# Ninety-six unused bytes at the end of SBUF, under a causal attention kernel in fp32 pairs

## The chip, the cores and the metric

The kernel runs on one core of one Trainium2 chip. The metric is the device time of one launch in microseconds (us), as the median of several runs. The engines are PE (matmuls, with PEld for its weight loads), DVE (VectorE), ACT (ScalarE), POOL (GpSimd) and SP (SyncE, which here only issues DMAs).

## The reference

The input is one sequence of 2048 tokens of 512 values. After a layer norm, a multi-head latent attention with 16 heads is computed, and a gated linear layer with eight low-rank experts; the two results are multiplied and added to the input:

```python
xn = _layernorm(x, axis=-1)
s = _L0_attn_ref(xn, W_DQ, W_UQ, W_QR, W_DKV, W_UK, W_UV, W_KR, W_O)   # 16 heads, 128 + 64 rotary, causal, scores clipped to +-80
g = _silu(_L0_ffn_ref(xn, weight, lora_A, lora_B, router_w))          # base layer + top 2 of 8 experts of rank 16
x = x + s * g
```

Inside the attention, per head: scores = q k^T with q and k of 128 + 64 values, softmax over the keys up to the token's own, times v (the latent of 128 values stands for both k and v), then the output projection W_O.

## The kernel before, in words

Every fp32 operand of a matmul is split into a high and a low part (names ending in `_h` and `_l`), and each product is three matmuls: high by high, high by low, low by high.

Three phases follow each other.

1. `prepare` (the first 150 us or so) normalizes x, makes latents, keys, values and the linear layer. Its buffers lie on the left side of SBUF and are given back at its end.
2. The sweep, in `attend_and_combine`. The sixteen tiles of 128 query tokens are taken in eight couples of 256 tokens, and each couple in two units of eight heads: unit n = 2m + par is couple m, heads 0 to 7 (par 0) or 8 to 15 (par 1). A unit holds its queries as `q_h`, `q_l`, `rot_hh`, `rot_l0`, each 128 x 2048, and walks over its key tiles: first the diagonal tile (CORNER), then the second diagonal tile (LATE), then 2m full tiles (FULL). Each key tile is one pair of halves (four heads each). In a half PE writes the scores, ACT takes the exponential (line 1415), DVE clips it (1540), ACT casts the high part (1421), DVE subtracts for the low part (1558) and adds to the row sums (1553), and PE multiplies with the values. PE works one pair ahead with the scores.
3. The projection (`project`, lines 1361 to 1363): 16 tiles of tokens, each 16 heads x 3 matmuls of 128 x 512, from about 1232 us to the end.

In FULL pairs the matmuls run as two at once, on the upper and the lower 64 rows of the array. One half is 15 such slots: nine for scores (line 1242, moving operands `q_h`, `q_l`, `q_h`, `rot_hh`, `rot_l` and then `q_h`, `q_l`, `q_h`, `rot_hh`) and six for the values (line 1264, moving operands `prob_h`, `prob_l`, `prob_h`, twice). CORNER and LATE use whole-array matmuls (lines 1212 to 1224 for scores, 1283 to 1287 for values). All of these stream 512 fp32 columns, 2048 bytes of each partition, except in LATE, where some stream 256.

```python
for n, (upper, lower, moving) in enumerate(blocks):
    for r, keys_of in enumerate((upper, lower)):
        c = 1 - r if crossed else r
        mm = pe.matmul(score_ps[:, half, c * 512:(c + 1) * 512], keys_of[ROWS[r], :],
                       moving[par][ROWS[r], half * HW + c * 512:half * HW + (c + 1) * 512],
                       start=n == 0 and not crossed, stop=n == len(blocks) - 1 and crossed)
```

The buffers of the two parities lie on different sides of SBUF. Those of par 0 (`q_h0`, `q_l0`, `rot_hh0`, `rot_l00`, `total0`) are in the class `Top`, on the right side; those of par 1 (`q_h1` and so on) are on the left. `merged_l`, one of the two moving operands of the projection, takes the place of the four query buffers of par 0 when the sweep ends; `merged_h` is on the left.

```python
q_h, q_l, rot_hh, rot_l0 = [top.q_h, q_h1], [top.q_l, q_l1], [top.rot_hh, rot_hh1], [top.rot_l0, rot_l01]
merged_h, merged_l = by_heads(keep.merged_h[:, :], DIM), by_heads(top.merged_l[:, :], DIM)
```

The right side is filled downwards from byte 229344 of each partition, which is 96 past a multiple of 128.

Of the kernel before, what the change touches and what calls it, by code (L numbers as in the profile page):

```python
# [18 lines left out]
F32 = mybir.dt.float32  # L19
F32R = mybir.dt.float32r  # L20

P = 128
# [51 lines left out]


WO_FIRST = 13


def homes(nc, ctx, side, words, sets):


    made = []
    for tensors in sets:
        with ExitStack() as lent:
            made.append([lent.enter_context(nc.sbuf_tensor(name, [P, width], dt, side=side)) for name, width, dt in tensors])
    ctx.enter_context(nc.sbuf_tensor("home_of_" + sets[0][0][0], [P, words], F32, side=side))
    return made


class Persistent:  # L90


    def __init__(self, nc, ctx):
        def sb(name, shape, dt):
            return ctx.enter_context(nc.sbuf_tensor(name, shape, dt))

        ((self.cos, self.sin, self.qr_h, self.qr_l), (self.wo_first,),
         (self.rows_h, self.rows_l, self.scale, self.x_in)) = homes(nc, ctx, "left", 2 * (SEQ + CT) + 4 * GT, (
            (("cos", SEQ + CT, F32), ("sin", SEQ + CT, F32), ("qr_h", 2 * GT, F32R), ("qr_l", 2 * GT, F32R)),
            (("wo_first", WO_FIRST * DIM, F32),),  # L100
            (("rows_h0", HQ, F32R), ("rows_l0", HQ, F32R), ("scale0", HQ, F32), ("x_in0", DIM, F32))))
        ((self.absorb_h, self.absorb_l, self.cq_h, self.cq_l),
         (self.merged_h, self.x_in1)) = homes(nc, ctx, "left", 2 * HQ + 2 * (SEQ + CT), (
            (("absorb_h", HQ, F32R), ("absorb_l", HQ, F32R), ("cq_h", SEQ + CT, F32R), ("cq_l", SEQ + CT, F32R)),
            (("merged_h", HEADS * DIM, F32R), ("x_in1", DIM, F32))))
        self.causal = sb("causal", [P, CT], F32)
        self.ones = sb("ones", [P, 32], F32)


class Top:  # L110
# [2 lines left out]

    def __init__(self, nc, ctx):

        self.head_rows = ctx.enter_context(nc.sbuf_tensor("head_rows", [P, HQ], F32, side="right"))
        self.sums = ctx.enter_context(nc.sbuf_tensor("sums", [P, 512], F32, side="right"))
        (self.q_h, self.q_l, self.rot_hh, self.rot_l0), (self.merged_l,) = homes(nc, ctx, "right", 4 * HQ, (
            (("q_h0", HQ, F32R), ("q_l0", HQ, F32R), ("rot_hh0", HQ, F32R), ("rot_l00", HQ, F32R)),
            (("merged_l", HEADS * DIM, F32R),)))  # L120
        (self.total,), (self.rows,) = homes(nc, ctx, "right", HQ, ((("total0", HQ, F32),), (("rows0", HQ, F32),)))
# [701 lines left out]
def attend_and_combine(nc, keep, top, keys, values, turned, w_uv, w_o, heads_out, sums_out, inverses, x, linear, out):  # L823

    ctx = ExitStack()
    with ctx:
# [3 lines left out]
        def sem(name):  # L830
# [18 lines left out]
            (*((f"prod{n}", 512, F32) for n in range(4)), ("rot_f", 2 * 512, F32), ("rot_hl", 4 * 512, F32R)),  # L849
            (("wo_rest", (HEADS - WO_FIRST) * DIM, F32), ("uv", HEADS * LAT, F32)),  # L850
            (("rows1", HQ, F32), ("scale1", HQ, F32), ("lin_in0", DIM, F32), ("gate0", DIM, F32))))
# [8 lines left out]
        def by_heads(ap, width):  # L860

            return ap.rearrange("p (h n) -> p h n", n=width)

        wo_parts = [by_heads(keep.wo_first[:, :], DIM), by_heads(wo_rest[:, :], DIM)]
        wo = [wo_parts[h // WO_FIRST][:, h % WO_FIRST, :] for h in range(HEADS)]
        uv = by_heads(uv_flat[:, :], LAT)
# [859 lines left out]
```

## Time and profile before

| | |
|---|---|
| Median of 3 runs | 1421.35 us (1419.82 to 1422.22) |
| The profiled execution's own time | 1420.26 us |
| Its span, first to last instruction | 1418.7 us |
| Granted TensorE clock over the span | 0.994 |
| Busy: PE, PEld | 1381.4 us (97%), 1147.4 us (81%) |
| Busy: DVE, ACT, POOL | 1146.3 us (81%), 782.1 us (55%), 125.1 us (9%) |
| HBM read, written | 125.83 MB, 48.50 MB, 123 GB/s over the span |

Busy time is the union of an engine's instructions. Matmuls are pipelined, so that the one that follows starts while the one before is still in its recorded 0.39 us; the step from start to start says how fast PE goes, and the busy share doesn't.

### The profile page before, as it was taken

What the parts mean: (1) busy time and instruction counts of PE and PEld (TensorE: products, weight loads), DVE (VectorE), ACT (ScalarE), POOL (GpSimd) and SP (SyncE); (2) the same over time, 40 slices, a digit from 0 to 9 for tenths busy, and PEclk for the clock granted to TensorE, in tenths of its full rate; (3) what the DMA queues carried; (4) which work ended last, traced back from release to release, by engine and by line L of the source; (5) the groups of instructions that cost most, each with busy time, mean ns of one, the idle gap of its engine ahead of it and who ended that gap; (6) DMA issues with size and microseconds to landing.
All of it is one profiled execution on the core that took longest, in us unless ns stands there. A gap on an engine that the chain in (4) does not pass through costs nothing.

```text
span 1418.7 us, 27675 instructions
## 1 busy us (share of the span) xinstructions
PE 1381.4 (97%) x9810; PEld 1147.4 (81%) x9810; DVE 1146.3 (81%) x1339; ACT 782.1 (55%) x861; POOL 125.1 (9%) x175
## 2 busy tenths in 40 slices
PE   7999689999999999999999999999999999999998
PEld 6888568778888888888888889888899688878887
DVE  7666378898898898988889898898788888967664
ACT  4232367666666666666566665666665656533221
POOL 0000111101101101010010100111100011022121
PEclk9999899999999999999999999999999999999999
DMA  8322665645435423333242422444412233166552
GB/s 304 121 88 101 176 190 152 177 131 160 119 94 141 120 95 91 123 84 120 66 119 85 116 99 63 122 151 140 131 56 63 67 109 118 52 199 172 169 158 89
DMA packets 110769, 174.91 MB, mean 123 GB/s; under 512 B 9608, under 2 KB 65160, under 8 KB 108168
## 3 DMA queue, kind: packets, MB, share of 16 engines
q1 hardware_dynamic: 93880, 108.99, 25.1%
q0 software_dynamic: 16016, 63.80, 15.7%
q10 hardware_dynamic: 832, 1.57, 0.5%
q8 instruction: 26, 0.43, 0.1%
q14 instruction: 15, 0.12, 0.0%
HBM read 125.83 MB, written 48.50 MB: 123 GB/s over the span
## 4 chain that ended last, share of the span: by engine, by line
PE 74%; DVE 8%; ACT 3%; DMA 3%; issue 1%; POOL 0%; ACTq 0%; SPq 0%; DVEq 0%; POOLq 0%
PE score_ps L1242 29%; PE out_ps L1264 19%; PE score_ps L1361 3%; PE score_ps L1362 3%; PE score_ps L1363 3%; DVE prob_l L1558 2%; PE out_ps L1283 1%; ACT prob_h L1421 1%; PE out_ps L1284 1%; PE out_ps L1287 1%; PE score_ps L1212 1%; DMA rot_l<-turned 1%; DVE prob L1545 1%; DVE prod L1517 1%; PE score_ps L1213 1%
## 5 line engine op out<-in xcount | busy, mean ns | idle before, releaser
L1421 ACT CAST prob_h<-prob 128x1024 fp32r<-128x1024 f32 (+1 forms) x288 | 289.8, 1006 | 236.1 <-DVE prob L1540 188.7
L1558 DVE TENSOR_TENSOR prob_l<-prob,prob_h 128x1024 fp32r<-128x1024 f32 (+1 forms) x288 | 335.9, 1166 | 39.6 <-ACT prob_h L1421 38.2
L1415 ACT ACTIVATE prob<-score_ps 128x1024 f32<-128x1024 f32 (+1 forms) x288 | 281.8, 979 | 148.8 <-PE score_ps L1242 99.3
L1242 PE MATMUL score_ps<-q_h,key_slot 64*128 64x512 f32 x1792 | 363.7, 391 | 0.0
L1264 PE MATMUL out_ps<-prob_h,value_slot 64*128 64x512 f32 (+1 forms) x1792 | 348.7, 377 | 1.8 <-DMA value_slot<-values 1.0
L1553 DVE TENSOR_TENSOR total<-total,prob 128x1024 f32<-128x1024 f32 (+1 forms) x256 | 294.7, 1151 | 0.0
L1540 DVE TENSOR_SCALAR prob<-prob 128x1024 f32<-128x1024 f32 x224 | 155.1, 692 | 72.0 <-ACT prob L1415 71.7
L1264 PEld LDWEIGHTS out_ps<-prob_h,value_slot 64*128 64x128 f32 x1792 | 178.3, 184 | 38.2 <-DVE prob_l L1558 6.6
L1242 PEld LDWEIGHTS score_ps<-q_h,key_slot 64*128 64x128 f32 x1792 | 178.2, 184 | 30.6 <-issue 5.0
L1242 PE MATMUL score_ps<-q_l,key_slot 64*128 64x512 f32 x896 | 181.1, 390 | 0.0
L1242 PE MATMUL score_ps<-rot_hh,key_slot 64*128 64x512 f32 x896 | 180.9, 389 | 0.0
L1264 PE MATMUL out_ps<-prob_l,value_slot 64*128 64x512 f32 (+1 forms) x896 | 174.7, 375 | 0.0
L1361 PE MATMUL score_ps<-merged_h,rows_h 128*128 128x512 f32 x256 | 101.1, 395 | 0.4 <-DVE rows_l L1568 0.4
L1362 PE MATMUL score_ps<-merged_l,rows_h 128*128 128x512 f32 x256 | 101.0, 395 | 0.0
L1242 PEld LDWEIGHTS score_ps<-rot_hh,key_slot 64*128 64x128 f32 x896 | 88.9, 184 | 14.3
L1363 PE MATMUL score_ps<-merged_h,rows_l 128*128 128x512 f32 x256 | 100.3, 392 | 0.0
L1264 PEld LDWEIGHTS out_ps<-prob_l,value_slot 64*128 64x128 f32 x896 | 89.3, 185 | 12.6
L1242 PEld LDWEIGHTS score_ps<-q_l,key_slot 64*128 64x128 f32 x896 | 89.0, 184 | 10.3
L1469 ACT CAST rows_h<-rows 128x1024 fp32r<-128x1024 f32 x32 | 33.7, 1052 | 109.9 <-DVE rows L1562 108.7
L1242 PE MATMUL score_ps<-rot_l,key_slot 64*128 64x512 f32 x448 | 90.3, 389 | 0.0
L1545 DVE SCALAR_TENSOR_TENSOR prob<-prob,causal 128x1024 f32<-128x1024 f32 (+1 forms) x64 | 61.0, 953 | 16.5 <-ACT prob L1415 16.2
L1507 DVE TENSOR_TENSOR q_l<-score_ps,q_h 128x1024 fp32r<-128x1024 f32 x32 | 37.8, 1219 | 27.8 <-ACT q_h L1386 27.8
(210 smaller groups left out, 2000.5 us busy)
## 6 DMA issues: line engine op xcount, KB each, us to landing
key_slot<-keys SPq DMA_DIRECT2D x144, 256.0 KB, 2.7
value_slot<-values SPq DMA_DIRECT2D x144, 128.0 KB, 2.3
rot_hh<-turned POOLq DMA_DIRECT2D x30, 512.0 KB, 6.2
heads_rows<-head_rows POOLq DMA_DIRECT2D x15, 1024.0 KB, 9.7
turned<-rot_hl POOLq DMA_DIRECT2D x14, 1024.0 KB, 5.2
rows<-heads_rows SPq DMA_DIRECT2D x28, 512.0 KB, 5.8
rot_l<-turned POOLq DMA_DIRECT2D x30, 256.0 KB, 7.7
x_in<-in_x SPq DMA_DIRECT2D x16, 256.0 KB, 2.7
```

The lines of the kernel that those rows point to most:

```text
L1242: mm = pe.matmul(score_ps[:, half, c * 512:(c + 1) * 512], keys_of[ROWS[r], :], moving[par][ROWS[r], half * HW + c * 512:half * HW + (c + ...
L1264: mm = pe.matmul(out, values_of[ROWS[r], :], moving, start=False, stop=False)
L1361: pe.matmul(sum_ps[par], rows_h[par][:, h, :], merged_h[:, h, :], start=(h == 0), stop=False)
L1362: pe.matmul(sum_ps[par], rows_h[par][:, h, :], merged_l[:, h, :], start=False, stop=False)
L1363: mm = pe.matmul(sum_ps[par], rows_l[par][:, h, :], merged_h[:, h, :], start=False, stop=(h == HEADS - 1))
L1415: nc.scalar.activation(prob[half][:, 0:width], score_ps[:, half, 0:width], ACT.Exp, scale=QK_SCALE).then_inc(exp_done, 1)
L1421: nc.scalar.copy(prob_h[half][:, 0:width], prob[half][:, 0:width]).then_inc(high_done, 1)
L1507: nc.vector.tensor_tensor(q_l[par][:, cols], score_ps[:, half, :], q_h[par][:, cols], ALU.subtract).then_inc(q_split, 1)
L1540: nc.vector.tensor_scalar(p, p, P_MIN, P_MAX, ALU.max, ALU.min).then_inc(clipped, 1)
L1545: nc.vector.scalar_tensor_tensor(out=heads, in0=heads, scalar=P_MIN, in1=limit, op0=ALU.max, op1=ALU.min).then_inc(clipped, 1)
L1553: nc.vector.tensor_tensor(sums, sums, by_head(half, kind), ALU.add).then_inc(summed, 1)
L1558: nc.vector.tensor_tensor(p_l, p, p_h, ALU.subtract).then_inc(split, 1)
```

## The change

The class `Top` reserves 24 fp32 words (96 bytes) per partition at the very end of the right side, before its other buffers. Nothing reads or writes them.

```diff
 WO_FIRST = 13
+EDGE = 24
...
     def __init__(self, nc, ctx):
 
+        ctx.enter_context(nc.sbuf_tensor("edge", [P, EDGE], F32, side="right"))
         self.head_rows = ctx.enter_context(nc.sbuf_tensor("head_rows", [P, HQ], F32, side="right"))
```

Every buffer on the right side then begins 96 bytes lower. The instruction lists of the two built programs are the same on every engine and in the same order, with the same waits; only the addresses of these buffers differ. The addresses, as the two builds place them (bytes in a partition), beside those of the left side that work with them:

| buffer | before | modulo 128, 256 | after | modulo 128, 256 |
|---|---|---|---|---|
| `head_rows` | 221152 | 96, 224 | 221056 | 0, 128 |
| `q_h0` | 210912 | 96, 224 | 210816 | 0, 128 |
| `q_l0` | 202720 | 96, 224 | 202624 | 0, 128 |
| `rot_hh0` | 194528 | 96, 224 | 194432 | 0, 128 |
| `rot_l00`, `merged_l` | 186336 | 96, 224 | 186240 | 0, 128 |
| `total0`, `rows0` | 178144 | 96, 224 | 178048 | 0, 128 |
| `q_h1`, `q_l1`, `rot_hh1`, `rot_l01` (par 1) | 87296 + 8192 k | 0, 0 | same | 0, 0 |
| `prob_h`, `prob_l`, `key_slot`, `value_slot` | | 0, 0 | same | 0, 0 |
| `merged_h` | 43136 | 0, 128 | same | 0, 128 |
| `w_h`, `w_l` in `prepare`, columns of chunk c | | 32 c | same | 32 c |
| `b_h`, `b_l` in `prepare` | 183936, 185984 | 0, 128 | same | 0, 128 |

## Rows read from the trace of the kernel before

**Rows 1.** The page, parts 1 and 2: busy us per engine, and granted clock by slices.

```profile
PE 1381.4 (97%) x9810; PEld 1147.4 (81%) x9810; DVE 1146.3 (81%) x1339; ACT 782.1 (55%) x861; POOL 125.1 (9%) x175
...
PEclk9999899999999999999999999999999999999999
```

**Rows 2.** The page, part 4: share of the chain that ended last, by engine.

```profile
PE 74%; DVE 8%; ACT 3%; DMA 3%; issue 1%; POOL 0%; ACTq 0%; SPq 0%; DVEq 0%; POOLq 0%
```

**Rows 3.** Busy us by stretch: PE, PEld, DVE, ACT, POOL, granted clock, DMA share, GB/s.

```profile
816.00:894.00 78.00, 77.97 (x676) 69.76 (x674) 69.65 (x71) 47.55 (x47) 1.00 (x1) 1.00 0.24 78
913.00:990.00 77.00, 76.88 (x681) 62.77 (x681) 68.99 (x72) 47.70 (x48) 11.28 (x20) 1.00 0.49 155
1290.00:1400.00 110.00, 110.00 (x477) 89.38 (x477) 73.83 (x71) 26.97 (x30) 23.35 (x10) 1.00 0.57 166
```

**Rows 4.** Exponentials (L1415) of units 12, 13, 14, 15: ns min/median/max, first and last start.

```profile
L1415 ACT ACTIVATE prob<-score_ps x10: 593/1026/1030, 797.0 to 832.4; 128x1024 f32<-128x1024 f32 x8, 128x512 f32<-128x512 f32 x2
L1415 ACT ACTIVATE prob<-score_ps x18: 1025/1027/1028, 835.8 to 894.9; 128x1024 f32<-128x1024 f32 x18
L1415 ACT ACTIVATE prob<-score_ps x10: 592/1026/1029, 898.3 to 933.5; 128x1024 f32<-128x1024 f32 x8, 128x512 f32<-128x512 f32 x2
L1415 ACT ACTIVATE prob<-score_ps x18: 1023/1027/1029, 936.9 to 994.5; 128x1024 f32<-128x1024 f32 x18
L1415 ACT ACTIVATE prob<-score_ps x18: 1026/1027/1031, 1024.7 to 1084.0; 128x1024 f32<-128x1024 f32 x18
L1415 ACT ACTIVATE prob<-score_ps x18: 1026/1029/1031, 1149.9 to 1207.7; 128x1024 f32<-128x1024 f32 x18
```

**Rows 5.** Timeline of PE in unit 12 (par 0), one half: start, duration us.

```profile
849.99 0.42 PE L1242 MATMUL score_ps<-q_h,key_slot 64*128 64x512 f32 x2
...
853.48 0.42 PE L1242 MATMUL score_ps<-q_h,key_slot 64*128 64x512 f32 x2
```

**Rows 6.** Timeline of PE in unit 13 (par 1), one half.

```profile
950.74 0.39 PE L1242 MATMUL score_ps<-q_h,key_slot 64*128 64x512 f32 x2
...
954.14 0.39 PE L1242 MATMUL score_ps<-q_h,key_slot 64*128 64x512 f32 x2
```

**Rows 7.** Timeline of PE where the last values follow on a projection tile.

```profile
1243.12 0.40 PE L1362 MATMUL score_ps<-merged_l,rows_h 128*128 128x512 f32 x1
...
1243.58 0.39 PE L1283 MATMUL out_ps<-prob_h,value_slot 128*128 128x512 f32 x1
...
1244.28 0.39 PE L1283 MATMUL out_ps<-prob_h,value_slot 128*128 128x512 f32 x1
...
1246.09 0.39 PE L1287 MATMUL out_ps<-prob_h,value_slot 128*128 128x512 f32 x1
```

**Rows 8.** Matmuls of line 1362 from 1271 us on: ns min/median/max, first and last start.

```profile
L1362 PE MATMUL score_ps<-merged_l,rows_h x208: 392/393/398, 1270.6 to 1414.2; 128*128 128x512 f32 x104
```

**Rows 9.** Costliest DVE groups, 919 to 996 us: busy us, mean ns, idle us before.

```profile
L1558 DVE TENSOR_TENSOR prob_l<-prob,prob_h 128x1024 fp32r<-128x1024 f32 x23 | 28.2, 1225 | 0.5 <-ACT prob_h L1421 0.5
L1553 DVE TENSOR_TENSOR total<-total,prob 128x1024 f32<-128x1024 f32 x22 | 26.8, 1218 | 0.0
L1540 DVE TENSOR_SCALAR prob<-prob 128x1024 f32<-128x1024 f32 x23 | 15.9, 692 | 6.3 <-ACT prob L1415 6.3
```

**Rows 10.** Timeline of PE in `prepare`, the matmuls that stream `b_h` and `b_l`.

```profile
76.42 0.40 PE L415 MATMUL base_ps<-b_h,turn_h 128*128 128x512 f32 x1
76.66 0.40 PE L416 MATMUL base_ps<-b_h,turn_l 128*128 128x512 f32 x1
...
78.29 0.40 PE L417 MATMUL base_ps<-b_l,turn_h 128*128 128x512 f32 x1
```

**Rows 11.** Casts into `q_h` of all units: ns min/median/max, first and last start.

```profile
L1386 ACT CAST q_h<-score_ps x32: 1002/1028/1042, 151.9 to 1006.9; 128x1024 fp32r<-128x1024 f32 x32
```

**Rows 12.** Landing of the `rot_l` gather: into par 1 (issued 369 us), into par 0 (428 us).

```profile
DMA to landing us min/median/max: 7.6/7.8/7.9
...
DMA to landing us min/median/max: 7.8/8.0/8.2
```

## The prediction, made before the changed kernel was run

> **What bounds the kernel now.** I read the page first. PE is busy for 97% of the span, DVE for 81% and the others less, and the clock is granted in full but for the beginning [rows 1]. The chain that ended last is PE for 74% of the span; DVE is the next with 8% [rows 2]. So the time of most of the kernel is the number of matmuls times the step from one to the next, and I looked for a difference in that step that could go with an address.
>
> The kernel holds an experiment of its own. Units of par 0 and of par 1 do the same work on the same shapes; the queries of par 0 lie on the right side, at 96 past a multiple of 128, and those of par 1 on the left, at multiples of 256. The stretches of unit 12 (par 0) and unit 13 (par 1) both have the full clock of 1.00, the higher of the two levels, 2.4 GHz, and PE is busy in all of both [rows 3]. Yet a half of unit 12 takes 853.48 - 849.99 = 3.49 us [rows 5] and one of unit 13 954.14 - 950.74 = 3.40 us [rows 6]. A half is 15 slots, so the step is 0.2325 us against 0.2267 us. It isn't one lucky half: over 17 halves the exponentials follow each other every (894.9 - 835.8) / 17 = 3.476 us in unit 12 and (994.5 - 936.9) / 17 = 3.388 us in unit 13, and it comes again as (1084.0 - 1024.7) / 17 = 3.488 and (1207.7 - 1149.9) / 17 = 3.400 us in units 14 and 15 [rows 4]. The difference is 0.088 us per half in both pairs of units.
>
> What else could differ between the units? DVE and ACT have the same work in both (69.65 and 68.99 us of DVE in stretches of 78 and 77 us), and par 1 has the busier DMA and is the faster one [rows 3]. What is left is where the moving operands of nine of the 15 slots lie. The values' slots, whose operands are the same in both units, must be slower too in par 0: the 0.09 us over 15 slots is more than I would place on any single one. I read this as a pace. PE falls into an even step of 0.2267 us when every operand begins at a round address, and never does when some don't.
>
> The place where the last values follow on a projection tile shows the pace setting in. The projection alternates `merged_h` (at 0 modulo 128) and `merged_l` (at 96) and steps by 0.23 us; the values that come right behind it (all at round addresses) start with such a step and then take eight steps from 1244.28 to 1246.09, 0.226 us each [rows 7]. These are whole-array matmuls, so the pace isn't a matter of the two at once. The projection itself never reaches it: 208 matmuls of line 1362 from 1270.6 to 1414.2, three slots each, give 143.6 / 621 = 0.2312 us per slot [rows 8], with PE busy in 110.00 of 110.00 us [rows 3].
>
> **The change part by part.** No instruction, wait or transfer is added, removed or moved, and the unused buffer costs nothing, as nothing touches it. All that can change is how long accesses to the moved buffers take.
>
> *Scores in par 0.* After the change the queries of par 0 are at 0 modulo 128. If their units then go as those of par 1, each half that PE paces gains 0.088 us. The first ten halves of a unit (CORNER, LATE and the first six of FULL) are nearly the same in both: from the first exponential to the eleventh 835.8 - 797.0 = 38.8 us in unit 12 and 936.9 - 898.3 = 38.6 in unit 13 [rows 4]. They are paced by the handing over between engines, and give 0.2 us per unit. Unit 2m has 4m halves of FULL; the first six don't count, which leaves 2, 6, 10, 14 and 18 for m = 2 to 6, or 50. Unit 14 is at its steady rate earlier, from the third or fourth half of FULL: 28 less 3, or 25. So 75 halves x 0.088 = 6.6 us, and 0.2 us for each of m = 3 to 7, or 1.0, where I take unit 14 as the others. Sum 7.6 us; I round it to 7.5. Were all 112 halves of FULL in par 0 paced by PE, it would be 9.9 us; that is the upper bound.
>
> What would be late next if PE is faster here is DVE. It has 1225 + 1218 + 692 = 3135 ns per half [rows 9], under the 3.40 us of a half in par 1, where the same work already goes at that rate; in that stretch it idles 6.3 us for ACT. So the gain isn't given back.
>
> *The projection.* 16 tiles x 48 = 768 slots. With both `merged_h` and `merged_l` at 0 modulo 128, and all weights too, the step can go from 0.2312 to 0.2267 us: 0.0045 x 768 = 3.5 us. PE is the pace there, DVE has 73.83 of 110 us and ACT 26.97 [rows 3].
>
> *The other users.* ACT and DVE write and read `q_h`, `q_l`, `total` and `head_rows` too. The 32 casts into `q_h`, half of them to each side of SBUF, lie between 1002 and 1042 ns [rows 11], so the side and the remainder are worth 40 ns each at most; they are inside the first halves of a unit, 14 of them to par 0 after the first, or 0.6 us if all of it were on the path. I take zero, nearest to the median of 1028. The gathers: the transfer of `rot_l` into par 1 lands after 7.6 to 7.9 us and that into par 0 after 7.8 to 8.2 [rows 12]. 0.2 us on two gathers that are on the chain early on is 0.4 at most; I take zero.
>
> The sum: 7.5 + 3.5 = 11.0 us, from the profiled execution's 1420.26 to 1409.3 us. That execution is 1.1 us under the median of the runs, so against the median of 1421.35 it is 1410.4 us.
>
> **What speaks against it: the rivals.** A change of 0.2% (2.8 us) is about what a measurement of this kernel can tell from none.
>
> *Nothing changes.* The parities also differ in the side of SBUF and in being at 0 or not modulo 256: every matmul of the trace that I saw in the even pace has all its operands at multiples of 256, and the right side is at 128 modulo 256 afterwards. The matmuls of `prepare` that stream `b_h` and `b_l`, both at 128 modulo 256, never settle in their groups of twelve: from 76.42 to 78.29 us eight steps of 0.234 us [rows 10], while the values in [rows 7] settled after three. This speaks for the rival; for my forecast speaks that their groups are short and come behind other shapes. The time would be 1421 us. The extra of the even step also hints at a granule: at 2.4 GHz 0.2267 us are 544 cycles for 512 columns, one more for each 16 columns or 64 bytes, an estimate worked out from [rows 6], and a multiple of 128 is a whole number of these.
>
> The Trainium skill (SBUF — State Buffer, Specifications) gives SBUF lines of 16 bytes, with a penalty for each crossing to a new line. 96 bytes are six whole lines, so by that rule no access crosses more lines before than after, and the time would stay. By that rule [rows 5] and [rows 6] would be alike too; the trace disagrees, with 3.49 against 3.40 us, as long as it is the address that sets them apart.
>
> *The sweep alone gains.* The projection has other weights for every matmul and another partner (`merged_h` at 128 modulo 256); if it doesn't settle, 1421.35 - 7.5 = 1413.9 us.
>
> *The projection alone gains.* If what counts is that all operands have the same remainder modulo 256, then `merged_h` and `merged_l` agree (128) and the queries of par 0 (128) and `prob` (0) don't: 1421.35 - 3.5 = 1417.9 us.
>
> *Slower.* A start at 128 modulo 256 could be the worse place. The longest steps that I found are in just such matmuls: 76.66 - 76.42 = 0.24 us [rows 10], against a mean of 0.2325. If the nine score slots of the 75 halves each took 0.24 in place of some 0.2335, it would be 9 x 75 x 0.0065 = 4.4 us, and the projection's 0.2312 going to the 0.234 of that group 2.2 us more: 1428 us. It decides from the point where a half of par 0 takes more than 3.49 us; 0.01 us on it is 0.75 us in all.
>
> **How the numbers follow.** Both gain: 0.62. Sweep alone 0.10, projection alone 0.08, nothing 0.14, slower 0.06. Predicted is the likeliest, 1410.4 us. Its own range is 1408 (all 112 halves) to 1413. The range that leaves out no more than nothing and slower, 0.20, is 1408 to 1418.5 us. The first three cases are all faster by over 0.2%: 0.80; same 0.14; slower 0.06.
>
> **What would show it.** Right: halves of units 10, 12 and 14 at 3.40 us; matmuls of line 1242 starting 0.226 to 0.227 us apart there as in unit 13; line 1362 at 0.68 us from one to the next in the projection in place of 0.693; units of par 1 as before; DVE and ACT durations as before. Wrong: if the halves of par 0 stay at 3.49, the remainder modulo 128 wasn't what set the parities apart, and modulo 256 or the side is; if the halves are at 3.40 and the time isn't lower, a wait has come in between units; and if units of par 1 change, whose addresses don't, the pace has another cause altogether.

## The result, and the profile after

Over 20 runs each, the median went from 1421.47 to 1418.89 us; the ratio is 0.9984, with a 95% interval of 0.9977 to 0.9991. One run of the kernel before was slow, at 1704.24 us, and the ratio leaves it out. The change made the kernel faster, by 0.16% by that ratio and by 2.6 us between the medians, where 11.0 were forecast. 1418.89 us is also 0.4 us outside the stated range. The profiled execution took 1419.24 us.

The page of the changed kernel, part 1, busy us of each engine:

```profile
PE 1381.3 (97%) x9810; PEld 1156.7 (82%) x9810; DVE 1144.5 (81%) x1339; ACT 781.9 (55%) x861; POOL 125.7 (9%) x175
```

PE is as busy as before to 0.1 us, and its share is 97% in both [rows 1]: the share says nothing about the step from one matmul to the next. Lines below 117 stand two numbers lower in the file now, so line 1415 of before is 1417 and 1362 is 1364.

The exponentials of units 12 and 13 in the changed kernel, over the same halves as in [rows 4] (columns: ns min/median/max, first and last start):

```profile
L1417 ACT ACTIVATE prob<-score_ps x18: 1025/1027/1032, 836.2 to 895.0; 128x1024 f32<-128x1024 f32 x18
...
L1417 ACT ACTIVATE prob<-score_ps x18: 1027/1027/1029, 937.0 to 994.7; 128x1024 f32<-128x1024 f32 x18
```

A half of unit 12 takes (895.0 - 836.2) / 17 = 3.459 us; it was 3.476. A half of unit 13 takes 3.394 us and hasn't changed. So par 0 got 0.017 us of the 0.088 that I had given it. One half of unit 12 on the timeline of PE:

```profile
850.34 0.42 PE L1244 MATMUL score_ps<-q_h,key_slot 64*128 64x512 f32 x2
...
853.81 0.41 PE L1244 MATMUL score_ps<-q_h,key_slot 64*128 64x512 f32 x2
```

3.47 us for 15 slots, 0.231 us each, where [rows 5] had 0.2325 and [rows 6] 0.2267.

The projection is the telling place. From 1271 us on its tiles were all alike, 392 to 398 ns a matmul and 0.2312 us a slot [rows 8]. Now the tiles of even number and those of odd number differ (even and odd are said of a tile's number here; the step of 0.2267 us is called the steady step). Line 1364 in one even and one odd tile (16 matmuls each, three slots from one to the next):

```profile
L1364 PE MATMUL score_ps<-merged_l,rows_h x16: 389/389/389, 1281.6 to 1291.8; 128*128 128x512 f32 x16
...
L1364 PE MATMUL score_ps<-merged_l,rows_h x16: 390/393/404, 1292.5 to 1302.9; 128*128 128x512 f32 x16
```

The even tile steps by (1291.8 - 1281.6) / 45 = 0.227 us; every one of its 16 has the same 389 ns. In the odd one they go from 390 to 404 ns, and the timeline gives its step:

```profile
1292.24 0.40 PE L1363 MATMUL score_ps<-merged_h,rows_h 128*128 128x512 f32 x1
1292.48 0.40 PE L1364 MATMUL score_ps<-merged_l,rows_h 128*128 128x512 f32 x1
...
1302.70 0.39 PE L1363 MATMUL score_ps<-merged_h,rows_h 128*128 128x512 f32 x1
```

45 slots take 1302.70 - 1292.24 = 10.46 us, 0.2324 each, where all tiles had 0.2312. The steady step is there in eight of 16 tiles, those of even number. What tells even tiles from odd ones is the buffer of the weights: `rows_h0` and `rows_l0` (16512 and 24704, both at 128 modulo 256) for even tiles, `rows_h1` and `rows_l1` (87296 and 95488, both at 0) for odd ones. The moving operands, `merged_h` and `merged_l`, are the same in both and now both at 128. In the odd tiles some steps are long, such as the 0.24 us from 1292.24 to 1292.48. [rows 10] had such a step too, and there too the moving operands were at 128 and the weights (`turn_h`, `turn_l`) at 0.

These rows gave the theory that the runs were to test. **Theory A:** PE falls into the steady step when the moving operand and the weights begin at the same remainder modulo 256, whatever that remainder is. Its rivals:

- **B**: the right side of SBUF is slower for PE.
- **C**: only the remainder modulo 128 counts (the forecast's own rule).
- **D**: the even tiles are fast for another reason in their buffers.
- **E**: only the moving operand's own start counts.
- **F**: agreement isn't enough, the common start must be round too.
- **G**: the two starts needn't agree, a short distance is enough.
- **H**: they need to agree modulo 64 only.

The accounts agree with the total: in the sweep 75 halves x 0.017 = 1.3 us; in the projection 384 slots x 0.0045 = 1.7 us gained in even tiles and 384 x 0.0012 = 0.5 us lost in odd ones. Sum 2.5 us, against 2.6 measured.

### The profile page after: what moved, and what is told of

Its sections match the earlier page's. It is cut to its first block, busy times and chain, and to the rows that moved or that the text cites. A ratio compares the mean times of both kernels' runs of the same rounds, so it can differ in the third digit from the quotient of the medians.

```text
span 1417.7 us, 27675 instructions
## 1 busy us (share of the span) xinstructions
PE 1381.3 (97%) x9810; PEld 1156.7 (82%) x9810; DVE 1144.5 (81%) x1339; ACT 781.9 (55%) x861; POOL 125.7 (9%) x175
## 4 chain that ended last, share of the span: by engine, by line
PE 72%; DVE 9%; ACT 3%; DMA 2%; issue 2%; POOL 0%; SPq 0%; DVEq 0%; ACTq 0%; POOLq 0%
PE score_ps L1244 29%; PE out_ps L1266 19%; PE score_ps L1363 3%; PE score_ps L1365 3%; PE score_ps L1364 3%; DVE prob_l L1560 3%; ACT prob_h L1423 2%; DVE prob L1547 1%; DVE prod L1519 1%; PE out_ps L1285 1%; PE out_ps L1289 1%; PE out_ps L1286 1%; DVE total L1555 1%; PE score_ps L1214 1%; PE score_ps L1215 1%
## 5 line engine op out<-in xcount | busy, mean ns | idle before, releaser
L1244 PEld LDWEIGHTS score_ps<-q_l,key_slot 64*128 64x128 f32 x896 | 90.5, 184 | 10.3
```

## The experiments

The kernels differ in unused bytes alone, and so in where the buffers begin. Where each puts what, modulo 256, and what it took (ratio to the kernel before, with its 95% interval):

| kernel | queries par 0, `merged_l` | key and value slots (weights) | `prob`, queries and rows par 1 | `merged_h`, rows par 0 | half of unit 12, 13 (us) | median us | ratio |
|---|---|---|---|---|---|---|---|
| before | 224 | 0 | 0 | 128 | 3.476, 3.388 | 1421.47 | |
| the change | 128 | 0 | 0 | 128 | 3.459, 3.394 | 1418.89 | 0.9984 [0.9977, 0.9991] |
| right_0 | 0 | 0 | 0 | 128 | 3.394, 3.388 | 1413.41 | 0.9942 [0.9928, 0.9955] |
| all_0 | 0 | 0 | 0 | 0 | 3.394, 3.388 | 1410.85 | 0.9926 [0.9912, 0.9939] |
| all_128 | 128 | 128 | 128 | 128 | 3.394, 3.388 | 1412.0 | 0.9926 [0.9913, 0.9940] |
| all_32 | 32 | 32 | 32 | 128 | 3.394, 3.388 | 1415.63 | 0.9958 [0.9945, 0.9972] |
| keys_128 | 0 | 128 | 0 | 128 | 3.476, 3.482 | 1429.07 | 1.0057 [1.0044, 1.0071] |

The kernels below were measured in three groups, each with the kernel before beside it: right_0, all_0, all_128 and all_32 (before: 1421.98 us); keys_128, right_32, right_64 and right_192, on another chip (1422.03); and the last three (1421.56). Each ratio goes by the kernel before of its group. The halves are worked out from the first and last start of 18 exponentials, rounded to 0.1 us, so they are good to 0.006 us.

**right_0: the right side at 0 modulo 256.** Edit:

```diff
-EDGE = 24
+EDGE = 56
```

> The unused buffer has 224 bytes in place of 96, so the right side begins at 0 modulo 256. Theory A (the even step of 0.2267 us needs moving operand and weights to begin at the same remainder modulo 256; key and value slots are at 0): halves of par 0 fall from 3.47 to 3.40 us, 7 us in all; in the projection merged_l (0) and merged_h (128) never both agree with the weights, so its even tiles of 10.9 us go back to 11.1 (384 slots of 0.0045 us, 1.7 us) and the odd ones stay near 11.1. Sum about 1421.4 - 7.5 = 1414 us. Rival B (right side of SBUF itself is slower for PE): halves of par 0 stay at 3.47, time 1419 to 1421. Rival C (only the remainder modulo 128 counts): as the change, 1419 us.

Units 12 and 13 of this kernel:

```profile
L1417 ACT ACTIVATE prob<-score_ps x18: 1026/1029/1031, 832.0 to 889.7; 128x1024 f32<-128x1024 f32 x18
...
L1417 ACT ACTIVATE prob<-score_ps x18: 1027/1028/1029, 931.6 to 989.2; 128x1024 f32<-128x1024 f32 x18
```

57.7 / 17 = 3.394 us in par 0 now, as in par 1, with the queries still on the right side: rival B has fallen, and so has C, since the step from 128 to 0 modulo 256 gave what the step from 96 to 0 modulo 128 had not. 1421.4 - 7.5 = 1414 us had been written down and 1413.41 were measured. That is 8.6 us under the kernel before beside it. The traces give less. All 288 exponentials, before and here:

```profile
L1415 ACT ACTIVATE prob<-score_ps x288: 590/1027/1033, 164.6 to 1232.4; 128x1024 f32<-128x1024 f32 x128, 128x512 f32<-128x512 f32 x16
...
L1417 ACT ACTIVATE prob<-score_ps x288: 589/1027/1032, 163.8 to 1224.8; 128x1024 f32<-128x1024 f32 x128, 128x512 f32<-128x512 f32 x16
```

From the first start to the last it is 1067.8 us before and 1061.0 here, so the sweep gained 6.8 us and the term was rightly sized to some 10%. The first exponential starts anywhere from 163.8 to 167.4 us in the traces of these kernels, a scatter that hides differences of 2 or 3 us in a single run. The projection's even tiles lost the steady step, as expected:

```profile
L1364 PE MATMUL score_ps<-merged_l,rows_h x16: 395/395/396, 1274.2 to 1284.7; 128*128 128x512 f32 x16
...
L1364 PE MATMUL score_ps<-merged_l,rows_h x16: 388/388/393, 1285.4 to 1295.7; 128*128 128x512 f32 x16
```

10.5 / 45 = 0.233 us in the even tile, where two matmuls of three agree with their weights and one doesn't, and 10.3 / 45 = 0.229 in the odd one, where one of three agrees. So the number of matmuls that agree doesn't give the step; mixed streams have steps of their own.

**all_0: everything at 0.** Edit, beside the one above:

```diff
+        sb("left_first", [P, 32], F32)
         ((self.cos, self.sin, self.qr_h, self.qr_l), (self.wo_first,),
...
         self.ones = sb("ones", [P, 32], F32)
+        sb("left_gap", [P, 32], F32)
```

> Right side at 0 modulo 256 and, by 128 unused bytes before and 128 after the buffers that outlive prepare, every operand of sweep and projection at 0 modulo 256 too. Theory A: halves of par 0 at 3.40 us (7.5 us), all 16 projection tiles at 10.9 us in place of 11.1 (3.5 us): 1410.5 us. Rival B (the right side is slower): no more than the projection's even tiles, 1417 to 1419 us. Rival D (even projection tiles go fast because of something else in their buffers): odd tiles stay at 11.1 and the time is 1412 us.

An even and an odd tile of its projection:

```profile
L1366 PE MATMUL score_ps<-merged_l,rows_h x16: 389/389/389, 1274.7 to 1284.9; 128*128 128x512 f32 x16
...
L1366 PE MATMUL score_ps<-merged_l,rows_h x16: 389/389/389, 1285.6 to 1295.8; 128*128 128x512 f32 x16
```

10.2 / 45 = 0.227 us in both, so D has fallen. The time is 1410.85 us, the fastest of all kernels here and nearly the 1410.4 that the forecast had given to the change. In this kernel `q_h0` is at 256 and the key slots at 0 modulo 512, so 512 isn't needed.

**all_128: everything at 128.** Edit: `EDGE` stays at 24, and

```diff
         self.ones = sb("ones", [P, 32], F32)
+        sb("left_gap", [P, 32], F32)
```

> The change as it is, and 128 unused bytes on the left before the buffers of the sweep, so that keys, values, queries, probabilities and rows all begin at 128 modulo 256. Theory A (only that they agree counts): par 0 and par 1 halves at 3.40 us and all projection tiles at 10.9 us: 1410.5 us. Rival E (a moving operand has to be at 0 modulo 256 by itself): neither parity reaches 3.40, the odd units lose 0.07 to 0.09 us on some 90 halves, 1424 to 1428 us.

Units 12 and 13:

```profile
L1418 ACT ACTIVATE prob<-score_ps x18: 1027/1029/1032, 835.9 to 893.6; 128x1024 f32<-128x1024 f32 x18
...
L1418 ACT ACTIVATE prob<-score_ps x18: 1027/1029/1029, 935.5 to 993.1; 128x1024 f32<-128x1024 f32 x18
```

Both at 3.39 us, and the projection, in an even and an odd tile:

```profile
L1365 PE MATMUL score_ps<-merged_l,rows_h x16: 389/389/389, 1277.6 to 1287.8; 128*128 128x512 f32 x16
...
L1365 PE MATMUL score_ps<-merged_l,rows_h x16: 389/389/389, 1288.4 to 1298.6; 128*128 128x512 f32 x16
```

A moving operand at 128 is as good as one at 0 once its weights are at 128 too; E has fallen for the first time. The ratio is the same as that of all_0, with 224 unused bytes in each partition where all_0 has 480. Here, in all_32 and in keys_128 the buffers of `prepare` move with the gap as well.

**all_32: the sweep at 32.** Edit: `EDGE = 48`, and `sb("left_gap", [P, 8], F32)` at the same place.

> Keys, values, queries, probabilities, rows of par 1 and merged_l all at 32 modulo 256; rows of par 0 and merged_h stay at 128. Theory A in its pure form (only agreement counts, not roundness): halves of both parities at 3.40 us, projection tiles of both kinds mixed, at 11.1 to 11.2: about 1414 us. Rival F (agreement and a multiple of 64 or 128 are both needed): no half at 3.40, both parities at 3.47 to 3.49, some 1428 us. Some buffers of prepare move by 32 bytes as well, worth under 1 us.

```profile
L1418 ACT ACTIVATE prob<-score_ps x18: 1028/1029/1029, 834.1 to 891.8; 128x1024 f32<-128x1024 f32 x18
...
L1418 ACT ACTIVATE prob<-score_ps x18: 1028/1029/1029, 933.7 to 991.3; 128x1024 f32<-128x1024 f32 x18
```

3.394 and 3.388 us, with every operand of the sweep 32 bytes past a multiple of 256. Roundness is worth nothing; F has fallen.

**keys_128: the same queries, other weights.** `EDGE = 56`, the `left_gap` of all_128, and behind the slots the same gap again, so that of the sweep's buffers only they move modulo 256 (those behind move by 256 bytes):

```diff
         value_slot = [sb(f"value_slot{n}", [P, SV], F32R) for n in range(2)]
+        sb("after_slots", [P, 32])
```

> Every moving operand of the sweep at 0 modulo 256 in both parities, but the key and value slots (all the weights) at 128. Theory A (weights and moving operand have to agree modulo 256): no unit is even, halves of par 1, whose queries have not moved, go from 3.40 to 3.46 us as those of par 0; 150 halves x 0.07 = 10 us more than with the slots at 0, so 1413.4 + 10 = some 1424 us, slower than before. Rival E (only the moving operand's own start counts): halves stay at 3.40 and the time at 1413 us.

```profile
L1419 ACT ACTIVATE prob<-score_ps x18: 1024/1027/1031, 842.2 to 901.3; 128x1024 f32<-128x1024 f32 x18
...
L1419 ACT ACTIVATE prob<-score_ps x18: 1025/1026/1029, 943.4 to 1002.6; 128x1024 f32<-128x1024 f32 x18
```

3.476 and 3.482 us: par 1 has lost its pace, though its queries and probabilities begin where they always did modulo 256. E has fallen again. This is the strongest of the runs: of the matmul operands of sweep and projection, modulo 256, nothing but the place of the five slots differs from right_0, and 1413.41 us became 1429.07, more than before the change. The 1424 us had been worked out with 0.07 us a half, from a unit whose value slots agree; with the 0.088 measured here it is 150 x 0.088 = 13.2 us on 1413.4, or 1426.6. The trace has the rest:

```profile
L1419 ACT ACTIVATE prob<-score_ps x288: 589/1027/1032, 166.9 to 1242.5; 128x1024 f32<-128x1024 f32 x128, 128x512 f32<-128x512 f32 x16
```

That is 1075.6 us from the first exponential to the last, in place of right_0's 1061.0: the sweep lost 14.6 us. The first exponential came 3.1 us later than in right_0, which is inside the scatter of the kernels whose `prepare` buffers haven't moved (163.8 to 167.1 us), so it isn't shown to come of the change.

**right_32, right_64, right_192: which differences count.** `EDGE` 48, 40 and 8, nothing else.

> Right side at 32 modulo 256, slots at 0. Theory A: halves of par 0 not even, between 3.45 and 3.50 us in unit 12. A rival G, that the two only have to start within a short distance, would have them at 3.40. Time 1419 to 1423 against 1413 us.

> Right side at 64 modulo 256, slots at 0. Theory A with 256 as the period: halves of par 0 not even, 3.45 to 3.50 us. Rival H, a period of 64 (which the difference of 128 in the change speaks against already): 3.40. Time 1418 to 1422 us under A.

> Right side at 192 modulo 256, slots at 0. Theory A: halves of par 0 not even, 3.45 to 3.50 us in unit 12, as with 64; time 1418 to 1422 us. Gives one more point of how the step depends on the difference of the remainders.

Unit 12 of right_32:

```profile
L1417 ACT ACTIVATE prob<-score_ps x18: 1027/1028/1029, 838.8 to 897.8; 128x1024 f32<-128x1024 f32 x18
```

of right_64:

```profile
L1417 ACT ACTIVATE prob<-score_ps x18: 1025/1028/1029, 835.9 to 895.1; 128x1024 f32<-128x1024 f32 x18
```

and of right_192:

```profile
L1417 ACT ACTIVATE prob<-score_ps x18: 1024/1027/1029, 834.7 to 894.0; 128x1024 f32<-128x1024 f32 x18
```

By the distance of the queries of par 0 from the key slots modulo 256, a half takes 3.394 us (0), 3.471 (32), 3.482 (64), 3.459 (128), 3.488 (192) and 3.476 (224, before). Only 0 is steady; the others differ by 0.03 us among each other, and 128 is the least bad. G and H have fallen. The times are 1421.35 us (ratio 0.9993, 0.9983 to 1.0004), 1420.8 (0.9996, 0.9986 to 1.0006) and 1420.04 (0.9997, 0.9987 to 1.0007), none different from before. Distances of 96 and 160 weren't tried for the queries, nor any under 32 bytes, so how closely the two must agree is known to 32 bytes and no better.

**projection_only and sweep_only: the change in two.** In the first `merged_l` goes to its new place and the queries stay; in the second the queries go and `merged_l` stays at 224. `total0` and `rows0`, which lie below it, go with `merged_l` in both, so the first kernel doesn't move it quite alone, as its expectation has it.

```diff
-            (("merged_l", HEADS * DIM, F32R),)))
+            (("merged_pad", 24, F32), ("merged_l", HEADS * DIM, F32R))))
```

The edit shown is that of projection_only. The room that `merged_l` shares with the queries is made 24 words longer for it and `EDGE` is 0; sweep_only keeps `EDGE = 24` and has 40 words in both places.

> The kernel before with merged_l alone at its place of the change (128 modulo 256); the queries of par 0 stay at 224. Theory A: even projection tiles, whose rows are at 128 as merged_h and merged_l are, step by 0.2267 us, odd ones by 0.2324: 384 x 0.0045 less 384 x 0.0011, or 1.3 us less in the projection; units as before. Time 1420.5 us or a little less.

> The change with merged_l (and total0, rows0) put back at 224 modulo 256; the queries of par 0 at 128. Units of par 0 as in the change (halves at 3.46 us in unit 12, 1.2 us in all), the projection as before (0.2312 us a slot). Time 1420.5 us or a little less.

> The change itself, on the same chip as the two that take it apart: as its first measurement, 0.9984 of before, some 1419 us; even projection tiles again at 0.2267 us and odd ones at 0.2324, halves of par 0 again at 3.46 us in unit 12.

An even and an odd projection tile of projection_only:

```profile
L1363 PE MATMUL score_ps<-merged_l,rows_h x16: 389/389/389, 1283.2 to 1293.4; 128*128 128x512 f32 x16
...
L1363 PE MATMUL score_ps<-merged_l,rows_h x16: 390/393/404, 1294.1 to 1304.6; 128*128 128x512 f32 x16
```

and of sweep_only:

```profile
L1364 PE MATMUL score_ps<-merged_l,rows_h x16: 398/398/398, 1282.6 to 1293.0; 128*128 128x512 f32 x16
...
L1364 PE MATMUL score_ps<-merged_l,rows_h x16: 392/392/395, 1293.7 to 1304.1; 128*128 128x512 f32 x16
```

In the first kernel the even tile has 10.2 / 45 = 0.227 us with 389 ns throughout, and the odd one 10.5 / 45 = 0.233 with 390 to 404 ns, as in the change; in the second both have 10.4 / 45 = 0.231. The steps come apart as expected. The times do so less sharply: projection_only 1420.33 us (ratio 0.9990, 0.9981 to 0.9999), sweep_only 1418.9 (0.9980, 0.9971 to 0.9989), the change again 1419.04 (0.9979, 0.9970 to 0.9988). By the middle values the projection is worth 1.4 us and the sweep 2.8; the near end of the second interval is 1.6 us, a little more than the 1.2 expected. Together they would be 4.2 us where the change has 3.0 beside them. Runs of one kernel spread over 3 to 5 us, so the medians can't settle the division; the traces do it better. From the first exponential to the last it is 1067.8 us before, 1067.5 in projection_only, 1066.4 in sweep_only and 1066.1 in the change; from there to the end of the span 186.3, 185.1, 186.1 and 185.6. So the sweep gained 1.4 to 1.7 us where the queries moved and 0.3 where they didn't, and the projection 0.7 to 1.2 where `merged_l` moved and 0.2 where it didn't. The change run again has the steps of its first measurement: a half of unit 12 at (895.9 - 837.1) / 17 = 3.459 us, and the projection at the steady step in the even tile (1291.98 - 1281.78 = 10.20 us for 45 slots, 0.2267).

## Why the prediction was wrong, by its own steps

**What bounds the kernel: right.** PE's step sets the time of the sweep and the projection. When the step of par 0 went to 0.2267 us in right_0, 6.8 of the 7.5 us came in the trace's sweep (8.6 between the medians), and when both places had it in all_0, the 11.0 us came: 1410.85 against 1421.98 beside it, and against the 1410.4 that had been worked out. Nothing gave the gain back; DVE had the slack that [rows 9] said.

**What sets the parities apart: wrong, and this is the step that failed.** The prediction says of the queries of par 0 "After the change the queries of par 0 are at 0 modulo 128. If their units then go as those of par 1", and of the projection "With both `merged_h` and `merged_l` at 0 modulo 128, and all weights too". The rule behind both, an even step "when every operand begins at a round address", isn't what the runs show. What counts in them is that the moving operands and the weights begin at the same remainder modulo 256. The change took the distance from 224 to 128, from one wrong value to a less wrong one, and a half of par 0 stayed at 3.46 us, near the 3.49 that the prediction had named as its sign of being wrong. Every stretch at the steady step that I found in the trace before had all its operands at 0 modulo 256, so it could not tell roundness from agreement, nor 128 from 256.

**Scores in par 0.** 0.088 us x 75 had been expected; 0.017 x 75 = 1.3 us came. The count of halves was right to about a tenth: at 0.088 us in right_0 the sweep's 6.8 us stand against 7.6, and the first ten halves of unit 12 gave 0.1 us (832.0 - 793.3 = 38.7 against 38.8) where 0.2 a unit had been taken from unit 13.

**The projection.** 3.5 us had been expected; 1.2 came: 1.7 from eight of 16 tiles, less 0.5 in the others. I had treated the weights as one group ("and all weights too"), and the two parities of the rows differ modulo 256.

**The rivals.** "Nothing changes" and "the projection alone gains" had named the remainder modulo 256, and had the second half of the truth: "If what counts is that all operands have the same remainder modulo 256, then `merged_h` and `merged_l` agree (128) and the queries of par 0 (128) and `prob` (0) don't". That one, at 0.08, is nearest to what happened, in the number by some luck: its 1417.9 us is 3.5 us in the projection and nothing in the sweep, and 1.2 and 1.3 came. It missed that the weights of odd tiles don't agree and that the wrong distances aren't worth the same. The rows that spoke for it, [rows 10], should have had more weight: eight steps in a stream at 128 with weights at 0, and one of 0.24 us among them, were the signature that the odd tiles show now. In "slower" the mechanism (a start at 128 is worse) is what the odd tiles do, by 0.0012 us a slot.

**The covers and the other users: right.** The casts into `q_h` take what they took:

```profile
L1388 ACT CAST q_h<-score_ps x32: 1002/1028/1041, 153.8 to 1007.1; 128x1024 fp32r<-128x1024 f32 x32
```

That is [rows 11] to 1 ns. So for these casts the remainder of what ACT writes doesn't matter. DVE's 1144.5 us of busy time against 1146.3 shows no cost there either.

**The Trainium skill's lines of 16 bytes** (SBUF — State Buffer, Specifications) were rightly set against the trace. By that rule all kernels here would be alike, as all distances are multiples of 16; the runs have 1410.85 to 1429.07 us, and the measurement decides.

**What stays open.** The rule is shown at the distances tried; its cause in the chip isn't. The traces have the weight loads overlapping the matmuls (in the change PEld 1156.7 and PE 1381.3 us busy in a span of 1417.7). That two reads at once go faster when they keep the same phase would be a natural story, but no run here tests it. Whether it is a matmul's own weights or those loaded during it that must agree can't be told from these kernels, where all weights of a stretch have one remainder or the step is mixed anyway. For the same reason it isn't known whether neighbouring matmuls may each agree at a remainder of their own. Streams of 256 columns and `prepare`, whose `w_h` chunks lie 32 bytes apart modulo 256 and so can't agree with anything as laid out, weren't tried.

## What to carry to other kernels

In a kernel bound by the step from one matmul to the next, lay out the weights and the moving operands so that they begin at the same remainder modulo 256 in a partition: it cost 480 unused bytes here and gave 0.74%, and all_128 had the same ratio for 224. To find out, compare the step (starts on the timeline, not busy time) between stretches that do the same work from other buffers, and write the addresses of both operands beside it. When all the good cases in a trace share several properties, the trace can't say which of them does it: a forecast should then split its chance between them, or the change should satisfy them all.

## What was not expected of the hardware

- Agreement of start addresses modulo 256 between weights and moving operand is worth 2 to 3% of a step of 512 fp32 columns: 0.2267 us against 0.231 to 0.233 (halves of 3.459 to 3.488 us in the sweep; 0.2312 in the tiles of before and 0.233 in the even ones of right_0), for whole-array matmuls and for two at once on 64 rows each. The granted clock was 1.00 in all these stretches.
- The common remainder itself is worth nothing: 0, 32 and 128 gave 3.39 us a half alike.
- Unused bytes can cost: 128 before and 128 behind the five slots took right_0 from 1413.41 to 1429.07 us, 1.1%.
- The page's busy share of PE can't show such a gain: it is 97% before, in the change and in all_0, whose time is 10.5 us less by its ratio. The busy time itself did fall in all_0, from 1381.4 to 1371.2 us, but not in the change (1381.3).
